# A recurrent layer and a mixture of experts on one core: the step recast as four cycles of four first layers and two second layers, ReLU in halves, all engines reordered

## What is computed

```python
h = tok(x)                                   # 64 pixels -> 64 features, + bias
h = h + rnn(layernorm(h))                    # h_t = tanh(W_ih x_t + b + W_hh h_{t-1}), t over the 16 images
# ffn(u) with u = layernorm(h):
logits = u @ gate_w + gate_b                 # 16 experts
w, idx = softmax of the top 2 logits
hid = relu(u @ w1[e] + b1[e])                # 64 -> 128, every expert e
eo  = hid @ w2[e] + b2[e]                    # 128 -> 64
y   = u + sum over the two chosen of w * eo
h = h + layernorm(y) * gamma + beta
```

## Time and profile before

| | |
|---|---|
| median of 3 runs | 512.27 us (511.43 to 512.4) |
| profiled execution | 511.07 us, of which the span is 509.0 us |
| PE busy | 492.6 us, 97% of the span |
| PE's share of the chain that ended last | 88% |
| DVE busy | 448.2 us, 88% |
| ACT busy | 342.9 us, 67% |
| POOL busy | 184.1 us, 36% |
| granted TensorE clock | 0.992 of full over the span |

### The profile page before, as it was taken

One profiled execution on the slowest core, in us unless ns is written; L12 is line 12 of the kernel. 1 busy time (PEld: TensorE's weight loads), 2 busy tenths in 40 slices (PEclk: granted clock), 3 DMA queues, 4 the chain that ended last, 5 costly groups with the idle time before them and its releaser, 6 DMA issues.

```text
span 509.0 us, 8784 instructions
## 1 busy us (share of the span) xinstructions
PE 492.6 (97%) x2982; PEld 322.7 (63%) x2982; DVE 448.2 (88%) x881; ACT 342.9 (67%) x586; POOL 184.1 (36%) x137
## 2 busy tenths in 40 slices
PE   8889999999999999999999999999999999999993
PEld 5565666666667666666666666666666666666652
DVE  1678888989989898998989999999989899999775
ACT  1556766859576785867678586766858676665652
POOL 3220304436161542726144352505345362222133
PEclk9989999999999999999999999999999999999998
DMA  6229292938549292866729294483918476582911
GB/s 141 80 72 221 64 217 68 223 96 189 139 96 216 72 220 64 178 147 131 180 53 221 80 206 121 111 202 91 232 30 192 119 154 143 122 190 56 223 36 32
DMA packets 31067, 69.04 MB, mean 136 GB/s; under 512 B 6720, under 2 KB 10800, under 8 KB 30896
## 3 DMA queue, kind: packets, MB, share of 16 engines
q1 hardware_dynamic: 31024, 68.49, 58.6%
HBM read 60.39 MB, written 8.08 MB: 135 GB/s over the span
## 4 chain that ended last, share of the span: by engine, by line
PE 88%; DVE 3%; DMA 2%; issue 2%; SPq 1%; POOL 1%; ACT 1%; POOLq 0%; DVEq 0%; ACTq 0%
PE pZ L911 38%; PE pO L928 35%; PE pA L863 2%; PE pA L830 2%; PE pA L942 2%; PE pA L853 2%; PE pA L880 2%; DMA gbias<-gate_b 1%; PE pB L892 1%; PE pA L843 1%; PE pB L942 1%; PE pB L880 1%; PE pA L854 1%; POOL inv_std L366 1%; DMA spread<-gates_dram 1%
## 5 line engine op out<-in xcount | busy, mean ns | idle before, releaser
L503 ACT ACTIVATE hexp<-pZ,b1c 128x784 f32<-128x784 f32 x256 | 221.4, 911 | 108.7 <-PE pZ L911 108.7
L928 PE MATMUL pO<-hexp,w2s 128*64 128x392 f32 x1024 | 198.4, 504 | 0.5 <-ACT hexp L503 0.3
L911 PE MATMUL pZ<-xt,w1hi 128*128 128x392 f32 x512 | 188.8, 369 | 0.0
L679 DVE SCALAR_TENSOR_TENSOR prod<-pO,b2c,spread 128x392 f32<-128x392 f32 x256 | 150.0, 621 | 30.1 <-PE pO L928 27.9
L911 PE MATMUL pZ<-xt,w1lo 128*128 128x392 f32 x512 | 174.5, 341 | 0.0
L911 PEld LDWEIGHTS pZ<-xt,w1hi 128*128 128x128 f32 x512 | 96.6, 189 | 46.1 <-issue 19.6
L366 POOL TENSOR_TENSOR inv_std<-var,nhalf 112x7 f32<-112x7 f32 x48 | 81.5, 1705 | 105.2 <-DVE var L569 105.2
L928 PEld LDWEIGHTS pO<-hexp,w2s 128*64 128x64 f32 x1024 | 69.5, 136 | 75.6 <-issue 63.0
L695 DVE TENSOR_TENSOR acc<-acc,prod 128x784 f32<-128x784 f32 x111 | 111.7, 1006 | 0.1
L911 PEld LDWEIGHTS pZ<-xt,w1lo 128*128 128x128 f32 x512 | 97.0, 189 | 0.0
L379 POOL TENSOR_TENSOR h2b<-h2c,bet 112x448 f32<-112x448 f32 x15 | 17.0, 1134 | 162.5 <-DMA h2c<-h_dram 162.5
(11 more groups left out here) (114 smaller groups left out, 501.4 us busy)
## 6 DMA issues: line engine op xcount, KB each, us to landing
spread<-gates_dram SPq DMA_DIRECT2D x126, 392.0 KB, 9.2
h_dram<-h SPq DMA_DIRECT2D x16, 248.1 KB, 2.4
h2c<-h_dram SPq DMA_DIRECT2D x16, 248.1 KB, 8.8
out<-yo SPq DMA_DIRECT2D x15, 196.0 KB, 9.2
xcur<-x_in SPq DMA_DIRECT2D x16, 112.0 KB, 7.9
xcur<-x_in SPq DMA_DIRECT2D x16, 84.0 KB, 8.7
w1f<-w SPq DMA_DIRECT2D x2, 512.0 KB, 5.8
spread<-gates_dram SPq DMA_DIRECT2D x4, 196.0 KB, 3.8
```

Of the source, the lines that this page charges most:

```text
L503: nc.scalar.activation(hexp[u % RING][:, :].rearrange("p (b c) -> p b c", b=2), halves(pZ[u % 2]), ACT.Relu, bias=b1c[:, u:u + 1]).then_in ...
L679: nc.vector.scalar_tensor_tensor(out=prod[q % RING][:, b * HALF:(b + 1) * HALF], in0=halves(pO)[:, b, :], scalar=b2c[:, q:q + 1], in1=spre ...
L911: last = nc.tensor.matmul(halves(pZ[e % 2])[:, b, :], w[:, e, :], xt[par][:, b * HALF:(b + 1) * HALF], start=(k == 0), stop=(k == 1))
L928: last = nc.tensor.matmul(halves(pO)[k * D:(k + 1) * D, b, :], w2s[:, e, :], hexp[e % RING][:, b * HALF:(b + 1) * HALF], start=True, stop= ...
```

## The change

- **Cycles.** A step is four cycles. A cycle issues four first layers, then two second layers, of the same four experts; no second layer is carried into the next step any more. The small groups stand between first and second layers or between the two second layers: x2_turn and embed_turn in the first cycle, recur and hidden_turn in the second, embed_in and gates_turn in the third, sum_turn in the fourth. Steps 0 and 15 have bodies of their own.
- **Halves.** ReLU is two instructions of 392 columns. z_ready and h_ready count halves; a first-layer half waits for the ReLU of that half two experts before, a second-layer half for that half of its experts.
- **Closing.** It is spread over two steps. sum_turn, close_center and the square of step t-1 are at the end of body t, the rest (variance, rstd, `close_norm`, gamma, output) in body t+1, with a chain FINISH of its own. POOL holds add_beta back until second layer 2 of the step has half begun to arrive, and close_out until second layer 6 has.
- **Order** of ACT, DVE and POOL anew, shown below for steps in the middle.

```diff
@@ -146,12 +146,9 @@
         MIX = Chain("mix_stage", "square var rstd x2 hi lo turned_a turned_b xt_a xt_b")
         GATE = Chain("gate_stage", "scaled biased max1 hit1 ranked1 first1 best1 without "
                                    "max2 hit2 ranked2 first2 best2 diff exp den p1 p2 g1 g2 gates turned gt")
-        CLOSE = Chain("close_stage", "turned center_a center square var rstd norm gamma out")
+        CLOSE = Chain("close_stage", "turned center_a center square var rstd")
+        FINISH = Chain("finish_stage", "norm gamma out")
...
@@ -270,6 +267,8 @@
 
             def fetch_h2(s):
 
+                if not known(s, 1):
+                    sp.wait_ge(h2b_set, 2 * s)
...
             def body(t, par, experts=False, gate=False, mix=False, embed=False, close=False):
                 if embed and known(t + 4, STEPS):
                     load_x(t + 4)
-                if close:
-                    fetch_h2(t - 1)
+                if close and not known(t, 2):
+                    fetch_h2(t - 2)
                 if mix:
                     keep_h2(t + 2)
                 if gate:
                     spread_gates(t + 1, 1 - par)
+                if close and not known(t, 2):
+                    store(t - 2)
                 if known(STEPS - 1 - t, 1):
-
-                    sp.wait_ge(h2b_set, 2 * t)
+                    fetch_h2(t - 1)
                     fetch_h2(t)
-                if close:
                     store(t - 1)
 
             load_x(0)
...
+            def second_layer_begun(t, q):
+
+                pool.wait_ge(y_ready, 2 * (t * Q + q) + 1)
 
             def body(t, par, experts=False, gate=False, mix=False, embed=False, close=False):
-                if close:
-                    add_beta(t - 1)
+                late = close and not known(t, 2)
+                if late:
+                    rstd(CLOSE, t - 2, 2)
+                    second_layer_begun(t, 2)
+                    add_beta(t - 2)
+                if mix:
+                    rstd(MIX, t + 2, 1)
                 if embed:
                     bias_h1(t + 3, 1 - par)
-                if mix:
-                    rstd(MIX, t + 2, 1)
-                if close:
+                    rstd(EMBED, t + 3, 0)
+                if late:
+                    if not known(STEPS - 1 - t, 1):
+                        second_layer_begun(t, 6)
+                    close_out(t - 2)
+                if known(STEPS - 1 - t, 1):
                     rstd(CLOSE, t - 1, 2)
-                if embed:
-                    rstd(EMBED, t + 3, 0)
-                if close:
+                    add_beta(t - 1)
                     close_out(t - 1)
 
...
@@ -493,44 +506,89 @@
                 nc.scalar.activation(w1hi[:, some, :], w1f[:, some, :], ACT.Copy).then_inc(w1_high, 1)
 
             def relu(t, u):
+
                 n = t * E + u
-                act.wait_ge(z_ready, n + 1)
                 if known(n, 1):
                     act.wait_ge(experts_loaded, EXPERTS_LOADED)
-                if not known(n, RING):
-
-                    act.wait_ge(y_ready, t * E + 2 * (u // 2) - RING + 2)
-                nc.scalar.activation(hexp[u % RING][:, :].rearrange("p (b c) -> p b c", b=2),
-                                     halves(pZ[u % 2]), ACT.Relu, bias=b1c[:, u:u + 1]).then_inc(h_ready, 1)
+                for b in range(2):
+                    act.wait_ge(z_ready, 2 * n + b + 1)
+                    if not known(n, RING):
+                        act.wait_ge(y_ready, 2 * ((n - RING) // 2) + b + 1)
+                    nc.scalar.activation(hexp[u % RING][:, b * HALF:(b + 1) * HALF], halves(pZ[u % 2])[:, b, :],
+                                         ACT.Relu, bias=b1c[:, u:u + 1]).then_inc(h_ready, 1)
+
+            def first_body():
+                relu(0, 2)
+                relu(0, 3)
+                relu(0, 4)
+                keep_xn1t(2)
+                relu(0, 5)
+                new_hidden(2)
+                high_part(1)
+                relu(0, 6)
...
+                exp_gap(1)
+                square_h2(2)
+                for u in range(8, 12):
+                    relu(0, u)
+                keep_h1(3, 1)
+                keep_gt(1)
...
             def body(t, par, experts=False, gate=False, mix=False, embed=False, close=False):
-                for u in range(E):
-                    if experts and not (known(t, 1) and u < 2):
-                        relu(t, u)
-                    if gate and u == at(t, 1, first=7):
-                        keep_xt(t + 1, 1 - par)
...
-                    if mix and u == at(t, 9, first=11):
-                        square_h2(t + 2)
...
+                for u in range(0, 4):
+                    relu(t, u)
+                if gate:
+                    keep_xt(t + 1, 1 - par)
+                if mix:
+                    keep_xn1t(t + 2)
+                for u in range(4, 8):
+                    relu(t, u)
+                if mix:
+                    new_hidden(t + 2)
+                if gate:
+                    exp_gap(t + 1)
+                if not known(t, 2):
+                    close_norm(t - 2)
+                if mix:
+                    square_h2(t + 2)
+                for u in range(8, 12):
+                    relu(t, u)
+                if embed:
+                    keep_h1(t + 3, 1 - par)
+                if gate:
+                    keep_gt(t + 1)
+                if embed:
+                    square_h1(t + 3, 1 - par)
+                if mix:
+                    high_part(t + 2)
+                for u in range(12, 16):
+                    relu(t, u)
+                square(CLOSE, t - 1, "center", 2, cen[:, :, :])
...
@@ -694,46 +754,102 @@
                     sofar = acc[par][:, :]
                 nc.vector.tensor_tensor(acc[par][:, :], sofar, prod[q % RING][:, :], ALU.add).then_inc(summed, 1)
 
...
+                if mix:
+                    scale_h1(s, par)
+                add(t - 1, 5, 1 - par)
+                if gate:
+                    bias_logits(g)
+                    find_first(g)
+                product(t, 0, par)
+                add(t - 1, 6, 1 - par)
+                product(t, 1, par)
+                add(t - 1, 7, 1 - par)
+                if gate:
+                    find_second(g)
+                if not known(t, 2):
+                    norm_var(CLOSE, t - 2, 2)
+                add(t, 0, par)
+                product(t, 2, par)
+                if mix:
+                    add_state(s, par)
+                product(t, 3, par)
+                if gate:
+                    gate_weights(g)
+                if mix:
+                    norm_var(MIX, s, 1)
+                add(t, 1, par)
+                add(t, 2, par)
+                product(t, 4, par)
+                if mix:
+                    norm_scale(MIX, s, 1, x2[:, :, :], h2[:, :, 0:D])
+                product(t, 5, par)
+                add(t, 3, par)
+                if embed:
+                    norm_var(EMBED, a, 0)
+                if mix:
+                    low_part(s)
+                add(t, 4, par)
+                product(t, 6, par)
+                close_center(t - 1)
+                product(t, 7, par)
...
@@ -904,23 +1018,23 @@
                     pe.wait_ge(h1_kept, 2 * 1 + 2)
                 if known(n, 2) and not known(n, 1):
                     pe.wait_ge(h1_kept, 2 * 2 + 2)
-                if not known(n, 2):
-                    pe.wait_ge(h_ready, n - 1)
                 for b in range(2):
+                    if not known(n, 2):
+                        pe.wait_ge(h_ready, 2 * (n - 2) + b + 1)
                     for k, w in enumerate((w1hi, w1lo)):
                         last = nc.tensor.matmul(halves(pZ[e % 2])[:, b, :], w[:, e, :],
                                                 xt[par][:, b * HALF:(b + 1) * HALF], start=(k == 0), stop=(k == 1))
-                last.then_inc(z_ready, 1)
+                    last.then_inc(z_ready, 1)
 
             def second_layer(t, q):
 
                 n = t * Q + q
-                pe.wait_ge(h_ready, 2 * n + 2)
                 if known(n, 1):
                     pe.wait_ge(w2_centred, 1)
                     pe.wait_ge(b2_centred, 1)
                     GATE.wait(pe, 0, "gt")
                 for b in range(2):
+                    pe.wait_ge(h_ready, 2 * (2 * n + 1) + b + 1)
                     if not known(n, 1):
                         pe.wait_ge(p_ready, 2 * n - 1 + b)
                     for k in range(2):
...
+            def first_body():
+                for u in range(2, 4):
+                    first_layer(0, u, 0)
+                second_layer(0, 0)
+                first_layer(0, 4, 0)
+                embed_turn(2)
+                first_layer(0, 5, 0)
+                recur(2)
+                for u in range(6, 8):
+                    first_layer(0, u, 0)
+                second_layer(0, 1)
...
+
+            def last_body():
+                t, par = STEPS - 1, (STEPS - 1) % 2
```

(37 more changed lines are left out.)

212 lines of the change are left out of this document (115 added, 97 removed).

## The result

The changed kernel takes **533.85 us** (median of 4 runs, 532.80 to 535.17) against 512.14 before (4 runs): ratio **1.0428**, 95% interval 1.0405 to 1.045. It is slower, by 21.7 us; the forecast of 509.1 and its whole range (505.0 to 513.6) were wrong. The profiled execution took 533.55, its span is 531.6 (before: 511.07 and 509.0).

What follows compares the result with a forecast made beforehand. TensorE's own stream was taken as the bound. Steps 1 to 12 -2.9, 13 to 15 -0.2, +0.1, -0.2, end -0.5, start +0.65: -3.1 us from 511.07, 508.0, given as 509.1 against the median; range 505.0 to 513.6.

Steps and rivals of the forecast that it cites:

- Bare cycle: TensorE's first and second layers without small groups: four cycles of joined runs save 1.35 us a step.
- small groups: The turns, recur and embed_in on TensorE, moved between other layers: together they cost 1.11 us more a step.
- rivals 3 and 4: Groups between second layers cost no more (495.8 or 502.5 us, chance 0.07); joining first layers saves nothing (515.5, chance 0.03).
- ScalarE in a run of four: Half ReLUs 0.405 us apart and 0.50 long in four first layers: no wait, by 0.04.
- Rival 1: Four first layers outrun ScalarE, the fourth's second half waits: 514.9 us at 0.45 spacing, 524 at 0.50; chance 0.14.
- Rival 2: B5, the step's sixth second layer, waits for product 4 as add_beta slows gate_weights: +3.9 us, 513.0; chance 0.10.
- Start: Step 0: four cycles -1.35 us and small groups -0.3 against stalls for late partners, together +0.65.
- Steps 13 and 14: Two of the last steps: -0.2 us for step 13, +0.1 for step 14.
- Direct second layers: A second layer directly behind another waits for VectorE's product: 1.79 us apart for 1.37, net 0.39 each.
- End: After the last step, last_sum_turn waits for one add less behind product 6: -0.5 us.
- VectorE: Add_beta and close_out held back on GpSimd give VectorE back 0.9 us a step; costed at 0 for its slack.
- SP: Gates ready at 21.5, wanted at 34.0; stores take 1.2 to issue, 2 to land, a spread 9.2: covered.

Runs made afterwards that it cites:

- a_nobias: The changed kernel with its half ReLUs without the bias column (b1 left out, still ReLU): 519.68 us.
- a_start2: The changed kernel with, in step 0, square_h2 behind ReLU 9, square_h1 and high_part behind ReLU 13, product 4 ahead of norm_var and two adds: 530.92 us.
- a_ideal2: The changed kernel without ReLU's bias column, step 0 and end reordered, product 4 ahead of add 2 and high_part behind ReLU 13 in steady steps: 512.33 us.
- a_best: The changed kernel with step 0 reordered, last close_norm behind ReLU 15, x2_turn inside the run, embed_turn waiting for keep_xt's first half only: 526.44 us.
- b_halves: The kernel before, in its old order, with ReLU in halves and its semaphores counted by halves: 514.29 us.
- a_start: The changed kernel with step 0's square_h2 moved from ahead of ReLU 8 to behind ReLU 9, nothing else: 531.19 us.
- a_copy: The changed kernel with each half ReLU replaced by a plain Copy of the same shape, without bias: 519.48 us.

## Why the prediction was wrong

- **Bare cycle and small groups** (-1.35 and +1.11 a step): right. Without ScalarE's delay an undisturbed step takes 29.26, forecast 29.24, and each cycle starts within 0.05 of its forecast; so rivals 3 and 4 fall. Joined first layers save what the hidden load of the earlier trace rows said. The Trainium skill's sentence that a weight load overlaps matmuls "only when row_grp differs" ("TensorE: Matmul & The Clock Gate", The mechanism), by which they would save nothing, doesn't hold here: matmuls 0.18 apart, each with a load of its own on the same 128 rows.
- **ScalarE in a run of four: the step that failed, with 14.2 of the 24.8 us between forecast and result.** I took the spacing of halves as half of a whole ReLU's 0.81, which leaves no room for a fixed cost, and its bounds, 0.34 to 0.45, from copies, which have no bias. Measured: 0.47 apart and 0.60 long, outside my bounds. Tanh with a bias column was in the same trace, 0.628 for a copy's 0.537; that was the row to take. The next ReLU follows a whole one after 0.797 at the least and a half one after 0.469, which makes 0.14 fixed and 0.84 ns a column. The Trainium skill ("ScalarE: Activation LUTs", What ACT_TABLE_LOAD costs) gives 280 ns + 0.833 ns a column with a bias column, 186 without: an estimate by these figures is 0.607 and 0.513 for 392 columns, and the traces have 0.601 and 0.523 in the mean (a_nobias). The page's overlap of two instructions, 93 ns, is too small here: 0.601 long and 0.469 apart is 0.13.
- **Rival 1** had the mechanism, at a chance of 0.14. Its formula, 3 x (0.47 - 0.405) - 0.04, gives 0.155 a cycle, since it holds a half's length at 0.50; with 0.60 it would be 0.255. TensorE lost 0.22, in two loads that were no longer hidden. And it left out that keep_xt and new_hidden stand behind the late ReLUs: embed_turn starts 0.08 later behind B0, and hidden_turn 1.78 behind B2 (1.64 in a_nobias, 1.47 forecast). Against a_nobias the four cycles are 0.28, 0.36, 0.23 and 0.23 longer: 1.10 a step.
- **Rival 2** (product 4) wasn't seen in the changed kernel. There gate_weights starts 16.25 after the step's start, when add_beta is nearly over, and takes 1.89 at most (1.40 alone). In a_nobias it starts at 15.6 and takes up to 2.87, and B5 was late by 0.3 to 1.0 in three steady steps. The mechanism was as described, but not in each step, and the 1.1 that I gave as its worst was 1.47.
- **Start:** I had +0.65 for step 0, with 2.29 for its stalls; it came to 6.05. I gave each wait a price of its own, and took into account neither what VectorE has to do behind h2, whose wait ends at 51.2 in a_start2 with no gap from there to 65, nor the clock behind idle time.
- **Steps 13 and 14:** as the steady ones, +1.1 each. **Direct second layers:** right, 1.80 apart for 1.79 in four of five (2.08 in one of step 14). **End:** 2.8 too little: ScalarE's spacing in four cycles (1.1), seven close_norms ahead of ReLU 12 (0.83 at first layer 14), and last_sum_turn 2.34 behind the last second layer, since the add that it waits for took 1.83 beside GpSimd's closing (1.77 behind and an add of 1.27 in a_ideal2, 1.47 and 0.98 in a_best). With all that mended, 36.9 for 36.6.
- **VectorE** 10 us less: right, 0.9 a step. **SP:** right, covered.

With ReLUs 0.09 cheaper and the queues of ScalarE and VectorE mended the change is a tie: in a_ideal2 steps 1 to 12 are 0.6 shorter than before, all twelve together. A net 0.24 a step was less than what the order asks of ScalarE and VectorE.

## What to carry to other kernels

Cutting an instruction in two doubled its fixed part here, so take the price of the half from an instruction with the same operands (a bias column, a scale column), not from half of the whole. When matmuls are put in longer runs on double buffers, ask the rate of the engine that empties them, and what stands behind its last one in its queue. A net gain of 0.24 a step out of two terms over 1 should be weighed against each partner's slack before it is believed.

## What the runs showed that I had not expected

- A bias column costs a ScalarE instruction 0.09 us (ReLUs 0.469 to 0.378 apart, 512 times; Tanh against a copy of its shape, 0.628 to 0.537 long). ReLU or Copy without it are the same.
- A weight load that waits 0.17 for a ReLU starts with its matmul and not beside the one before, and the next matmul then comes after 0.28 for 0.18.
- TensorE idle for 1.7 us at full clock was followed by 8 us at 0.57, some 3.4 us lost; in a_start, 1.71 idle by 0.54 and 0.61 over 4 us, 1.7 lost. In a_copy 2.09 idle was followed by full clock. An early stall of a partner can cost its own length in clock, or twice that, or nothing.
- GpSimd's rstd took 1705 ns in the mean before and in b_halves, 2201 in the changed kernel and 2203 in a_nobias. The three of a middle step took 1.49, 2.13 and 1.47 before and 2.15, 2.15 and 2.69 now. In the changed kernel nobody waits for it in steady steps; why it is longer in the new order wasn't tried.
